# Moving the layer norm's statistics and v's first half inside one batch of a two-layer graph kernel

## The reference, cut to what matters

```python
c_adj = mean(x over channels)                      # one number per node
A_s   = 2 * |(|sigmoid(c_adj[m] - c_adj[n]) - 0.5|) - 0.5|   # 1024 x 1024
g     = relu((x^T @ (adj * A_s)) * para)            # 256 x 1024
q     = g^T in 4 heads of 64;  k, v = (x @ kv_w) in 4 heads of 64
out_h = softmax(q_h k_h^T * scale) v_h              # per head, 1024 x 1024 scores
x     = layernorm(x + out)                          # over the 256 channels
```

## Time and profile before

| | |
|---|---|
| median of 3 runs | 2866.09 us (2864.56 to 2866.31) |
| the profiled execution's own time | 2866.0 us |
| its span | 2864.0 us |
| granted TensorE clock, mean over the span | 0.976 |
| PE busy | 2711.2 us (95%) |
| DVE busy | 1988.9 us (69%) |
| ACT busy | 1663.1 us (58%) |
| POOL busy | 1279.5 us (45%) |

### The profile page before, as it was taken

The page is one execution under the profiler, slowest core; times in us unless marked ns, Lnnn a source line. Parts: engine busy times, 40 slices in busy tenths (PEclk is TensorE's granted clock), DMA queues, the critical chain, the costliest instruction groups (busy, mean ns, idle before and its releaser), DMA issues. The chain is left out here.

```text
span 2864.0 us, 39358 instructions
## 1 busy us (share of the span) xinstructions
PE 2711.2 (95%) x12436; PEld 1850.8 (65%) x12436; DVE 1988.9 (69%) x2859; ACT 1663.1 (58%) x2146; POOL 1279.5 (45%) x684
## 2 busy tenths in 40 slices
PE   7999999999999999999999999996799999989964
PEld 5565665656656566665656656563688888878854
DVE  6687786877878687786877878784633333348878
ACT  6566576766667666576666767653422222237768
POOL 3755647565474755657566474745200000000025
PEclk9999999999999999999999999998899999999976
DMA  4123222232222232222232222220332223305556
GB/s 136 60 84 101 74 66 84 63 106 84 66 73 77 73 97 86 73 66 85 64 105 86 65 72 77 84 71 30 120 104 88 88 94 107 108 16 190 190 229 256
DMA packets 126943, 272.01 MB, mean 95 GB/s; under 512 B 11952, under 2 KB 62128, under 8 KB 123312
## 3 DMA queue, kind: packets, MB, share of 16 engines
q1 hardware_dynamic: 126896, 271.42, 29.4%
HBM read 178.79 MB, written 62.98 MB: 84 GB/s over the span
## 5 line engine op out<-in xcount | busy, mean ns | idle before, releaser
L303 POOL TENSOR_TENSOR psum<-psum,probs 128x1024 f32<-128x1024 f32 x320 | 784.3, 2451 | 144.2 <-ACT probs L373 118.1
L373 ACT ACTIVATE probs<-sc_ps 128x1024 f32<-128x1024 f32 x512 | 508.0, 1024 | 410.4 <-PE sc_ps L822 328.9
L552 DVE TENSOR_REDUCE mx<-mx_ps 128x1 f32<-128x512 f32 x768 | 520.2, 690 | 275.3 <-PE mx_ps L791 273.5
L838 PE MATMUL pv_ps<-probs,v 128*64 128x512 f32 x2048 | 492.4, 604 | 0.0
L822 PE MATMUL sc_ps<-qa,ka 128*128 128x512 f32 x1024 | 387.4, 404 | 0.0
L822 PE MATMUL sc_ps<-qb,kb 128*128 128x512 f32 x1024 | 380.6, 394 | 0.5
L791 PE MATMUL mx_ps<-ka,qa 128*128 128x512 f32 x768 | 315.4, 424 | 10.2 <-DVE mx L552 2.9
L838 PEld LDWEIGHTS pv_ps<-probs,v 128*64 128x64 f32 x2048 | 125.6, 136 | 224.5 <-issue 193.6
L822 PEld LDWEIGHTS sc_ps<-qa,ka 128*128 128x128 f32 x1024 | 187.5, 188 | 106.2 <-issue 64.1
L791 PEld LDWEIGHTS mx_ps<-ka,qa 128*128 128x128 f32 x768 | 139.8, 187 | 179.6 <-issue 77.9
L1177 DVE TENSOR_TENSOR agg_lo<-ag_ps,agg_hi 128x1024 fp32r<-128x1024 f32 x32 | 39.2, 1225 | 310.7 <-ACT agg_hi L1104 310.7
(11 more groups left out here) (195 smaller groups left out, 5548.2 us busy)
## 6 DMA issues: line engine op xcount, KB each, us to landing
adj_ring<-in_adj_dram SPq DMA_DIRECT2D x128, 512.0 KB, 3.7
pre_scratch<-pre SPq DMA_DIRECT2D x28, 1024.0 KB, 4.4
pre<-pre_scratch SPq DMA_DIRECT2D x28, 1024.0 KB, 4.9
x<-in_x_dram SPq DMA_DIRECT2D x16, 1024.0 KB, 5.6
kb<-ka SPq DMA_DIRECT2D x64, 256.0 KB, 3.1
res<-in_x_dram SPq DMA_DIRECT2D x16, 1024.0 KB, 5.6
x_scratch<-res SPq DMA_DIRECT2D x16, 1024.0 KB, 4.5
x1s<-x_scratch SPq DMA_DIRECT2D x16, 1024.0 KB, 7.5
```

The source lines that it names most:

```text
L303: pool.tensor_tensor(psum[:, h % 2, :], probs[:, 0, :] if k == 1 else psum[:, h % 2, :], probs[:, k % PR, :], ALU.add).then_inc(s["pool_ad ...
L373: nc.scalar.activation(probs[:, i % PR, :], sc_ps[:, t % 2, :], ACT.Exp, scale=SCALE)\
L552: nc.vector.tensor_reduce(mx2[:, nh, n:n + 1], mx_ps[:, nh, :], AX.X, ALU.max)\
L838: ins = nc.tensor.matmul(pv_ps[nh * HD:(nh + 1) * HD, h % 2, :], v[:, i, h * HD:(h + 1) * HD], probs[:, i % PR, nh * BANK:(nh + 1) * BANK] ...
```

## The change

Six edits, all in `attention_layer`:

1. DVE: `weigh(b, 7)` stands ahead of `add_head(b - 1, 3)` instead of behind it.
2. DVE: `row_stats` and `moments` leave the place ahead of `q_times_para`. Four tiles of the statistics stand between the maxima of tiles 0 to 3 and 4 to 6 of head 1, the other four and the moments between tile 6 and tile 7.
3. POOL: `rsqrt(b - 1)` leaves the head of the body and stands between the fourth and the fifth of head 0's adds. `q_low` waits for the adds of the batch before in its place.
4. ACT: `normalise` moves from pairs 0 and 1 of head 0 to pair 3 of head 0 and pair 0 of head 1.
5. PE and ACT: v's first half goes ahead of the k pieces, and `v_copy(b, 0)` ahead of `relu_q(b, 1)` and of `k_high`; of the next x's tiles three instead of two stand behind `v_copy(b, 1)`.
6. Head 1's maxima in head 0: `[0, 2, 1]` becomes `[0, 1, 1]`, and `[2, 1, 1, 1, 0]` becomes `[2, 1, 1, 1, 1]`; one half moves from the first pair to the end of the second.

```diff
-    MAX_HALVES = [[[0, 2, 1], [2, 1, 1, 1, 0], [2, 1, 1, 1, 1], [1, 1, 0, 0, 0]]] + \
+    MAX_HALVES = [[[0, 1, 1], [2, 1, 1, 1, 1], [2, 1, 1, 1, 1], [1, 1, 0, 0, 0]]] + \
...
+    LN_ADDS = 4
@@ gpsimd
-            def rsqrt(b):
+            def rsqrt(b, adds=LN_ADDS):
                 wait(pool, s["veps_done"], b + 1)
+                wait(pool, s["pool_added"], POOL_ADDS * 4 * (b + 1) + adds)
...
             def q_low(b, h):
                 if h == 0:
-                    wait(pool, s["rstd_done"], 2 * b)
+                    wait(pool, s["pool_added"], POOL_ADDS * 4 * b)
...
-                if not isinstance(b, int) or b > 0:
-                    rsqrt(b - 1)
+                before = not isinstance(b, int) or b > 0
...
+                        if before and (h, k) == (0, LN_ADDS + 1):
+                            rsqrt(b - 1)
+                            wait(pool, s["rstd_done"], 2 * b)
...
-            rsqrt(B - 1)
+            wait(pool, s["pool_added"], POOL_ADDS * 4 * B)
+            rsqrt(B - 1, 0)
@@ scalar
-                k_high(b, 2)
-                k_high(b, 3)
+                v_copy(b, 0)
                 relu_q(b, 1)
                 if not last:
                     x_high(b + 1, range(0, 2))
-                v_copy(b, 0)
+                k_high(b, 2)
+                k_high(b, 3)
                 if not last:
-                    x_high(b + 1, range(2, 6))
+                    x_high(b + 1, range(2, 5))
                 v_copy(b, 1)
                 if not last:
-                    x_high(b + 1, range(6, T))
+                    x_high(b + 1, range(5, T))
...
-                        if before and h == 0 and p < 2:
-                            normalise(b - 1, range(4 * p, 4 * p + 4))
+                        if before and (h, p) in ((0, 3), (1, 0)):
+                            normalise(b - 1, range(4 * h, 4 * h + 4))
@@ vector
+                weigh(b, 7)
                 if before:
                     add_head(b - 1, HEADS - 1)
-                weigh(b, 7)
                 w_low(b, 6)
                 w_low(b, 7)
-                if before:
-                    row_stats(b - 1)
-                if before:
-                    moments(b - 1)
...
-                maxima(b, 1, range(T))
+                maxima(b, 1, range(0, 4))
+                if before:
+                    row_stats(b - 1, range(0, 4))
+                maxima(b, 1, range(4, 7))
+                if before:
+                    row_stats(b - 1, range(4, T))
+                    moments(b - 1)
+                maxima(b, 1, range(7, T))
@@ tensor
                 g_product(b)
-                k_piece(b, 0, 0)
-                k_piece(b, 0, 1)
+                v_product(b, 0, [0, 1])
                 max_scores(b, 0, 0)
                 max_scores(b, 0, 1)
-                k_piece(b, 1, 0)
-                max_scores(b, 0, 2)
-                k_piece(b, 1, 1)
-                max_scores(b, 0, 3)
-                for m in range(4):
-                    v_product(b, 0, [m])
-                    max_scores(b, 0, 4 + m)
+                for n in (2, 3):
+                    v_product(b, 0, [n])
+                    max_scores(b, 0, n)
+                for n in range(4):
+                    k_piece(b, n // 2, n % 2)
+                    max_scores(b, 0, 4 + n)
                 v_product(b, 1, [0, 1])
                 transpose_maxima(b, 0)
-
                 v_product(b, 1, [2, 3])
```

More of the change, by code:

```diff
@@ L589, in add_head, with row_stats @@
                 last.then_inc(s["res_added"], 1)
-            def row_stats(b):
+            def row_stats(b, tiles=range(T)):
                 wait(dve, s["res_added"], 4 * b + 4)
-                for n in range(T):
+                for n in tiles:
                     nc.vector.bn_stats(stats[:, n, :], res[:, n, :]).then_inc(s["stats_done"], 1)
```

## The result

The changed kernel takes 2950.66 us (median of 4 runs, 2939.29 to 2957.03), the kernel before 2866.2 in the same comparison: ratio 1.0289, 95% interval 1.0271 to 1.0308. It is slower, as forecast, but by 84 us where 34 were forecast, and outside the range of 2880 to 2922. The profiled execution took 2944.33 us (span 2942.2, mean granted clock 0.972), 78 more than the profiled one of before: 5.2 us for each of 15 batches. The four runs differ by their clock too: the two short ones (2939 and 2944) have a mean granted clock of 0.972, the two of 2957 one of 0.966.

A forecast was written before the change was run, and what follows sets the result against it. PE was taken to set the batch, with POOL's chain of head 0's adds without slack. A middle batch grows 2.38 us, 33.3 over 14, plus 0.1 and 0.7: +34 on 2866.0, so 2900 us, range 2880 to 2922.

The forecast's parts named there:

- the forecast's own sign of being wrong: Prediction wrong if the batch is not over 123.5 us, or PE's longest wait in a batch stands elsewhere.
- weigh 7 idle: Edit 1: DVE idles ahead of weigh 7 for step 7's tanh, so `w_low(b, 6)` begins 0.76 us later.
- `q_times_para` bound by PE: Edit 2: it also needs PE's `g_first`, so of 3.69 us saved ahead only about 0.3 was on the path.
- the bubble's balance: Edits 1 and 5: PE reaches the transpose 0.23 us earlier, one more x_high costs 0.40, `split_x` begins 0.17 later.
- the statistics at full speed beside the adds: Head 0's pauses: `bn_stats` has one SBUF input, so the statistics cost their 2.71 us beside POOL's adds.
- the other 1.36 and the moments ... together 2.34, and so ends 0.7 late: Second DVE pause of head 0, 1.61 us long: half the statistics plus 0.98 us of moments end 0.7 late.
- 2.4 us more in each pause: Alternative bound for head 0's pauses: each half of the statistics sits out one POOL add, making PE late.
- the term of edit 3: rsqrt adds 2.21 us to head 0's adds; with 0.17, PE stalls 2.6 at half 4, batch 2.38 longer.
- I take nothing, and +0.5 as its upper end: Edit 4: later normalising and the later store in SP's queue cost nothing, at most 0.5 us a batch.
- up to 0.5 us late, with about 1 us to spare: Edit 4: head 2's row, made at about 963.4, may issue up to 0.5 us late, within about 1 us slack.
- the clock, a rival at 4%: PE's 2.6 us stall makes the clock fall each time, 2.6 us more a batch: 2939 us; chance 4%.
- The port rival: `add_last` loses the port to head 1's first POOL add and sits out 2.4 us: 2931 us; chance 10%.

The follow-up runs named there:

- the run that isolates it: Changed kernel with statistics and moments back ahead of `q_times_para` and head 1's first POOL add waiting for head 0's last: 2921.8 us, ratio 1.0194.
- the run with the sums moved: Changed kernel with `spread_sums(b + 1)` moved behind head 2's row (`store_row(b, 2)`) in SP's queue: 2913.7 us, ratio 1.0161.

## Why the prediction was wrong

The sign was right, but not for the reason given: the wait that was to make the kernel slower isn't there, and other waits are. In that it was luck. By the forecast's own sign of being wrong, PE's longest wait of a batch stands elsewhere (2.54 us for `mxs`). Four of its steps stand: weigh 7 idle (0.63 measured, 0.76 forecast; PE's wait at step 7 grew from 0.18 to 0.89), `q_times_para` bound by PE, the bubble's balance (edits 1, 5, 6 together +0.06%, within noise), and the statistics at full speed beside the adds.

**The step that failed first is "the other 1.36 and the moments ... together 2.34, and so ends 0.7 late".** The moments took 3.3 us, not 0.98, since `neg_mean` sat out an add. The prediction had the row that shows it (the 3.08 us at 994.10) and the rule, and applied both to `bn_stats` alone; the moments, in the same pause, have five instructions with two SBUF inputs and two `tensor_scalar` from SBUF. The bound of "2.4 us more in each pause" was written down and then dismissed, because the term of edit 3 would cover it. The two did cover each other: the last add was ready at 982.78 and `add_last`, held by DVE's own order, took it at 982.93. The forecast term of 2.38 us was true in size (2.96 us of stall in the run that isolates it, forecast 2.6) and made no wait of PE in the changed kernel, being hidden behind one that came earlier. In size the wait for `mxs`, 36.0 us over the span, only took the place of the 33.3 that were forecast. What carries the time out of the range are the next two steps.

**The second is "I take nothing, and +0.5 as its upper end"** for edit 4. It is 52 us alone, 37 in the changed kernel. For edit 4 alone the times in SP's queue came out right to 0.1 us. What was wrong was the slack: the 3.2 us from the row's issue to its use were not set beside PE's need of it 3.4 us after it is made, so "up to 0.5 us late, with about 1 us to spare" had almost nothing to spare. In the changed kernel the queue is later than forecast too: on the scale of before the store leaves at 951.6 and `cb` at 966.6, not at 948.2 and 963.2, while the row is made at 964.4. The second `normalise` stands behind head 1's first exponentials, and these need PE's scores, which the stall for `mxs` and the fall behind it had made 3.5 us late.

**The third is the clock, a rival at 4%.** It was judged by two gaps, 5.26 us with a fall and 2.11 without, as if one length decided. Repeated stalls of one length show that it doesn't: waits of 2.5 to 2.6 us had a fall in 6 of 14 batches of the changed kernel and in 10 of 14 of the run with the sums moved, waits of 2.96 to 3.0 us in 13 of 14, those of 5.0 in all 14, those of 1.6 to 1.7 in none of 15. The rival's price, 2.6 us for a fall, was too high for falls of 3.4 us, which cost 1.7 at most; and its 2939 counts 15 batches where the sum counts 14, which gives 2936.

**The port rival, at 10%,** came where it could, with the statistics back at g: `add_last` took 3.35 us and PE stood for 5.0, where 2.4 + 2.2 were forecast. The rival's time of 2931 is still 29 us under the 2960 measured; it leaves out the clock. It was argued wrong: the 0.16 us between adds is the wait of one add for the one before, and the first add of a head has no such wait. In the changed kernel it could not come, since head 1's first add itself waited 2.10 us for its exponentials.

What the 84 us are made of: 37 are the row's, by the run with the sums moved. The other 47, with edit 4's cost out, stand with 35.7 us of waits for `mxs` and ten falls of the clock, about 17 us; that the two are more than 47 together is left unexplained. That moments beside the adds cause such waits is shown by the two runs with moments or reduces added to the kernel before. In the changed kernel itself the trace has the 2.3 us of `neg_mean`, and the waits are gone when statistics and moments go back to g; the moments alone were not taken out of it. The runs' spread of 18 us (2939 to 2957) goes with the clock: 0.966 for 0.972 over 2950 us is about 18 us of full speed (an estimate). What makes the falls more in one execution than in another stays open; the row's wait varies from 1.2 to 2.5 us between batches of one execution.

## What to carry to other kernels

Before moving small VectorE work into a pause, look at what GpSimd does there and at the operands, not at the length: here an instruction with two SBUF inputs, or a `tensor_scalar` from SBUF, lasted as long as the rest of GpSimd's add. Look at the falls of the clock too, which no engine's wait shows. When a step is moved, move its DMA in the queue too, in thought, and ask what in-order entry behind it has a deadline; a wait for a transfer in the middle of a queue (`spread_sums`) makes every entry ahead of it dangerous. And a term that "covers" another is no reason to leave the other unpriced: work out which comes first.

## What the runs showed of the hardware

- VectorE and the large instructions of GpSimd (128x1024 and more) hold each other for whole instructions: 0.17 us became up to 2.37, a 1.22 us add 3.35 when GpSimd had begun 0.07 us earlier, and GpSimd's 2.39 became 3.31 when VectorE had begun 0.12 us earlier.
- A stall of PE of 2.5 us was followed by a granted clock of 0.50, from about 1.2 us after it resumed to 4.6 after; another of 2.58 us by 1.00 throughout. After one of 2.96 the first matmul already took 0.79 us, and the clock was at 0.50 for 3.4 us. The longer the stall, the more often it fell: 0 of 15 at 1.7 us, 6 of 14 and 10 of 14 at 2.5, 13 of 14 at 3.0, 14 of 14 at 5.0.
- The 4 KB of sums needed 8.0 us to complete behind 2.25 MB of other transfers (the residual, two adjacency tiles, a copy of k), and 1.4 us when issued later, behind the row alone (961.91 to 963.33 in the run with edit 4 and the sums behind the row).
